# Two mixtures of experts: routing each batch by itself beside the experts of the batch ahead

## The chip, the cores and the metric

The kernel runs on one core of one Trainium2 chip. The metric is the device time of one execution in microseconds (us); three executions of the kernel before took 819.97 us in the median (819.3 to 822.01).

## The reference, cut to what matters

The input is x, four batches of 512 tokens of 128 numbers. Four blocks are added to it in turn, each on a layer norm of x: a test-time-training attention, a mixture of experts, a softmax attention, and the same mixture of experts again. The change is in the two mixtures:

```python
def _L0_ffn_ref(x, We, be, Wg, bg):      # E = 8 experts, K = 2, D = O = 128
    x_flat = x.reshape(-1, d)
    gates = jax.nn.softmax(x_flat @ Wg + bg, axis=-1)
    topk_gates, topk_idx = jax.lax.top_k(gates, K)
    topk_gates = topk_gates / jnp.sum(topk_gates, axis=1, keepdims=True)
    expert_out = jnp.einsum('nd,edo->neo', x_flat, We) + be
    selected = jnp.take_along_axis(expert_out, topk_idx[:, :, None], axis=1)
    out = jnp.sum(selected * topk_gates[:, :, None], axis=1)
...
x = x + _L0_attn_a_ref(_layernorm(x, axis=-1), ...)
x = x + _L0_ffn_ref(_layernorm(x, axis=-1), ...)
x = x + _L0_attn_b_ref(_layernorm(x, axis=-1), ...)
x = x + _L0_ffn_ref(_layernorm(x, axis=-1), ...)
```

## The kernel before, in words

x lies on the chip the whole time, as 16 tiles of 128 tokens (a tile is 128 partitions of 128 numbers), four tiles to a batch. Every product that must be exact in float32 is made of three multiplications (`mm3`, L97 to L102): high part by high part, high by low, low by high. All experts are computed for every token, and each is weighted by a number that is zero for the six that were not chosen.

Each mixture is one call of `moe_phase` (L972 on), a program of its own between two barriers, in which each engine works through a list in the order of the code. It has these stages, each for all 16 tiles before the next begins:

- The norm. VectorE works out mean and inverse root (`ln_vector`, L387) with ScalarE's Sqrt in the middle (`ln_scalar`, L403), 16 tiles at once, then normalizes tile by tile (L1124). TensorE transposes four tiles at a time (L1076), ScalarE takes the high part out of the bank (L1054), VectorE the low part (L1130), and TensorE multiplies by the router's weights into 8 columns a tile (logits, 12 multiplications a batch at L100 to L102).
- The choice. When all logits are there, VectorE adds the bias (L1141), subtracts the largest, ScalarE takes Exp (L1057), and VectorE finds the best and second best by twice four or five operations on all 128 x 128 gates (L1150 to L1163). TensorE computes the experts of tiles 0 and 1 meanwhile.
- The biases. The weights of the experts are transposed (L1099), parted into high and low (L1059, L1165), and multiplied by the experts' biases, a 128 x 2048 matrix that holds them once per tile, into four banks (three multiplications of 512 columns each). VectorE adds each bank to x (L1169).
- The experts. For each tile TensorE does six multiplications of 512 columns into a pair of banks. There are four pairs in the eight banks, and a tile waits until the tile four before has left its pair. VectorE weights and sums experts 0 to 4 from the banks (L1187, five operations a tile, into two sums a and b), ScalarE scales experts 5 to 7 (L1066), GpSimd adds those up (L1043, L1045) and closes the tile with a + b (L1034). In the first mixture VectorE also takes the statistics of each closed tile for the next norm (L385). In the second, SyncE sends each finished batch out.

## Time and profile before

| what | us |
|---|---|
| median of 3 executions (lowest, highest) | 819.97 (819.3, 822.01) |
| the profiled execution's own time | 819.79 |
| its span, from the first to the last instruction | 818.0 |
| first mixture, from its first instruction to the last sum on VectorE | 346.2 to 402.0 |
| second mixture, the same | 760.6 to 814.8 |
| VectorE busy in the whole span | 519.8 |
| TensorE busy in the whole span | 753.3 |

The sum of the prediction is made against the profiled execution. Times within a mixture are told from its first instruction, at 346.2 or 760.6 us of the span. "Busy" of TensorE counts pipelined multiplications and their modelled ends, so it says little of how full the engine is. The granted clock of TensorE is given as a share of 2.4 GHz: 0.50 is the lower of its two levels (1.2 GHz), 1.00 the upper.

### The profile page before, as it was taken

The page shows a single profiled execution, that of the slowest core. Times are in us where ns is not written, and L with a number is a line of the kernel's source. Part 1 is how long each engine was busy: PE and PEld are TensorE (multiplying, and loading weights), DVE is VectorE, ACT ScalarE, POOL GpSimd, SP SyncE. Part 2 cuts the span into 40 slices and gives each one's busy share as a digit, 9 for nine tenths or more (in the row PEclk, how much of TensorE's full clock was granted, in tenths as well). Part 3 has the DMA queues.
Part 4 walks back from the last instruction along what each step waited for, and adds up shares of the span by engine and source line. Part 5 has one row for each costly group of instructions (what it writes and reads, how often), then busy time and mean ns, then how long its engine had stood idle before and what let it go on. Part 6 is the DMA issues. An engine that isn't in the chain of part 4 may idle for free. (4 is left out here: it accounts for less than half of the span.)

```text
span 818.0 us, 15239 instructions
## 1 busy us (share of the span) xinstructions
PE 753.3 (92%) x5432; PEld 601.2 (73%) x5432; DVE 519.8 (64%) x1570; ACT 382.7 (47%) x1080; POOL 266.6 (33%) x465
## 2 busy tenths in 40 slices
PE   5699999979999989888599999999999999999786
PEld 2389999859998878786357667777777777778764
DVE  5755555455555544457877777766766776664477
ACT  4533333543332362213457666655666655663224
POOL 5691000068000011004624444433334333442027
PEclk9799999999999999958889999999999999999679
DMA  8000000000000000000000000000000000000001
GB/s 249 4 0 2 1 1 1 2 0 2 1 1 1 2 1 1 1 1 0 1 1 2 1 2 1 2 2 2 2 2 1 2 1 2 1 2 2 1 0 52
DMA packets 9464, 7.15 MB, mean 9 GB/s; under 512 B 1584, under 2 KB 9008, under 8 KB 9264
## 3 DMA queue, kind: packets, MB, share of 16 engines
q1 hardware_dynamic: 9392, 6.19, 2.5%
q8 instruction: 45, 0.74, 0.4%
q14 instruction: 27, 0.22, 0.1%
HBM read 5.14 MB, written 1.05 MB: 8 GB/s over the span
## 5 line engine op out<-in xcount | busy, mean ns | idle before, releaser
L1324 POOL TENSOR_SCALAR t_p_<-t_p_,t_rinv_ 128x128 f32<-128x128 f32 (+3 forms) x256 | 132.5, 535 | 202.4 <-DVE t_rinv_ L1520 202.4
L1354 ACT ACTIVATE t_p_<-t_p_,t_nmin_ 128x128 f32<-128x128 f32 (+3 forms) x256 | 140.0, 551 | 9.6 <-DVE t_nmin_ L1513 9.6
L1513 DVE CUSTOM_DVE_ANT_0 t_p_<-t_S_,t_mask_ 128x128 f32<-128x128 f32 (+3 forms) x256 | 112.9, 488 | 21.6 <-PE t_S_ L1411 17.3
L1359 ACT ACTIVATE t_pT_<-t_T_ 128x384 f32<-128x384 f32 (+1 forms) x96 | 50.6, 527 | 118.2 <-PE t_T_ L1423 118.2
L1423 PEld LDWEIGHTS t_T_<-ident,t_p_ 128*128 128x128 f32 x640 | 68.2, 141 | 45.0 <-issue 26.1
L1411 PE MATMUL t_S_<-t_k_,t_q_ 64*128 64x256 f32 (+3 forms) x512 | 95.0, 468 | 0.1
L1423 PE MATMUL t_T_<-ident,t_p_ 128*128 128x128 f32 x640 | 90.8, 281 | 0.3 <-ACT t_pT_ L1359 0.3
L1438 PEld LDWEIGHTS t_O_<-t_pT_,t_v_ 128*64 128x64 f32 x1280 | 69.2, 137 | 11.0 <-ACT t_pT_ L1359 10.5
L1438 PE MATMUL t_O_<-t_pT_,t_v_ 128*64 128x128 f32 x1280 | 76.9, 275 | 0.0
L717 POOL TENSOR_TENSOR gvl<-gv,gvh 128x512 fp32r<-128x512 f32 x2 | 2.5, 1274 | 204.3 <-ACT gvh L824 204.3
L1411 PEld LDWEIGHTS t_S_<-t_k_,t_q_ 64*128 64x128 f32 x512 | 41.4, 185 | 26.9 <-DVE t_nmin_ L1513 12.3
L587 DVE SCALAR_TENSOR_TENSOR g_sw<-g_th,g_G 128x512 f32<-128x512 f32 x32 | 22.0, 688 | 59.4 <-ACT g_slope L465 29.9
L1524 DVE COPY t_pT_<-t_T_ 128x384 f32<-128x384 f32 (+1 forms) x96 | 57.3, 597 | 1.4 <-PE t_T_ L1423 1.3
L1529 DVE COPY t_oT_<-t_O_ 128x512 f32<-128x512 f32 x32 | 22.1, 692 | 54.8 <-PE t_O_ L1438 54.8
L1354 ACT ACTIVATION_READ_ACCUMULATOR t_p_<-t_p_,t_nmin_ 128x1 f32 x256 | 48.7, 190 | 0.0
L1066 ACT ACTIVATE m_y_<-m_A_,m_wt_ 128x128 f32<-128x128 f32 x96 | 28.1, 368 | 26.5 <-PE m_A_ L102 26.5
L469 ACT ACTIVATE g_hT<-g_H 128x512 f32<-128x512 f32 x32 | 19.1, 597 | 37.2 <-PE g_H L523 36.4
L610 DVE SCALAR_TENSOR_TENSOR g_du<-g_D,g_sw 128x512 f32<-128x512 f32 x32 | 22.1, 692 | 21.4 <-PE g_D L102 21.4
L530 PEld LDWEIGHTS g_PT<-proj,g_hT 128*128 128x128 f32 x256 | 33.7, 193 | 2.6
L550 PE MATMUL acc<-qkv,g_dg 128*128 128x128 f32 x256 | 34.0, 276 | 1.0 <-DVE g_dg L614 1.0
L530 PE MATMUL g_PT<-proj,g_hT 128*128 128x128 f32 x256 | 34.1, 276 | 0.0
L461 ACT ACTIVATE g_th<-g_G 128x512 f32<-128x512 f32 x32 | 19.1, 598 | 31.4 <-PE g_G L102 31.3
(254 smaller groups left out, 1707.3 us busy)
## 6 DMA issues: line engine op xcount, KB each, us to landing
wqkv<-in_L_attn_b_w_qkv_dram SPq DMA_DIRECT2D x1, 1536.0 KB
x<-in_L_attn_a_x_dram SPq DMA_DIRECT2D x4, 256.0 KB, 3.9
out_dram<-x SPq DMA_DIRECT2D x4, 256.0 KB, 2.3
we<-in_L_ffn_We_dram SPq DMA_DIRECT2D x1, 512.0 KB
wout<-in_L_attn_b_w_out_dram SPq DMA_DIRECT2D x1, 512.0 KB
gv<-n_L_attn_a_ttt_gate_dram SPq DMA_DIRECT2D x1, 256.0 KB, 4.8
gv<-in_L_attn_a_ttt_val_dram SPq DMA_DIRECT2D x1, 256.0 KB, 6.0
proj<-n_L_attn_a_ttt_proj_dram SPq DMA_DIRECT2D x1, 256.0 KB, 4.7
```

The costliest lines, as they stand in the source:

```text
L530: last = pe.matmul(pred, hT[:, t.ring, n * P:n * P + P], self.proj[:, n, :], start=(n == 0), stop=(n == NC - 1))
L550: last = pe.matmul(self.acc[:, n, m, :], src[:, t.ring, m * P:m * P + P], d[:, t.ring, :] if n == 2 else k, start=False, stop=False, skip_ ...
L610: dve.scalar_tensor_tensor(du[:, t.ring, :], psD[:, :], 0.5, sw[:, t.ring, :], ALU.mult, ALU.mult).then_inc(g["du"], 1)
L1066: last = act.activation(y[:, t % 4, tile_of(k)], experts_of(t, e), ACT.Copy, scale=weight(t, e))
L1324: last = pool.tensor_scalar(pr[:, G.par, h, cols], pr[:, G.par, h, cols], rinv[:, G.par, n:n + 1], 1.0, ALU.mult, ALU.mult)
L1354: act.activation(pr[:, G.par, h, cols], pr[:, G.par, h, cols], ACT.Exp, bias=nmin[:, G.par, n:n + 1], scale=-1.0, accum_out=rsum[:, G.par, ...
L1359: act.activation(pT[:, G.par, 0, G.blocks], psT[:, 0, 0:G.width], ACT.Copy).then_inc(t["eA"], 1)
L1411: last = pe.matmul(psS[:, (2 * G.n + h) % 3, at_:at_ + (qt + 1) * P], qp[d, G.par, qt * P:qt * P + P], kp[d, G.par, 0:(qt + 1) * P], start ...
L1423: last = pe.transpose(psT[:, h, k:k + P], pr[:, G.par, h, at_:at_ + P], ident[:, :])
L1438: last = pe.matmul(psO[d, qt * P:qt * P + P], v[:, G.b % 2, n, G.p * P + h * DH:G.p * P + h * DH + DH], pT[:, G.par, h, at_:at_ + P], star ...
L1513: dve.tensor_tensor_reduce(pr[:, G.par, h, cols], psS[:, (2 * G.n + h) % 3, at_:at_ + keys], mask[:, SEQ - keys:SEQ], 1.0, -NEG, ALU.add, ...
L1524: dve.tensor_copy(pT[:, G.par, 1, G.blocks], psT[:, 1, 0:G.width]).then_inc(t["eB"], 1)
```

## The change

`moe_phase` is replaced by `mixture_phase`, which makes a `Router` and an `Experts` object and walks all engines through one table of steps. The router works on one batch at a time: the norm's numbers on GpSimd with the power -0.5 (no Sqrt), the normalization on ScalarE, then transposes, high and low parts, logits, choice, weights and bias product of that batch. The choice goes by rank: all differences between two logits of a token are compared (8 x 8 per token, so 256 numbers a partition for a batch), a sum over them gives each expert's rank, and the shares of ranks 0 and 1 are 0.5 + 0.5 tanh(d/2) and 0.5 - 0.5 tanh(d/2) of the difference d of the two logits. The expert tiles follow FIRST = 7 steps later, one a step, in three pairs of banks; bank 7 is for the router's transposes and logits, bank 6 for weights and bias products. A tile's first half waits now until the tile three before has been summed through expert 3, the second until it has been summed through expert 4 and scaled. The experts' biases are held once per batch (32 x 512).

```diff
+class Router:
+    def norms(self, pool, b, ready):
+        st, w, of = self.k.stats, self.lnw, self.rows(b)
+        pool.wait_ge(*ready)
...
+        c(pool.tensor_tensor(self.rstd[:, of], w[:, 3, of], self.k.mhalf[:, 0:TPB], ALU.pow))
+        pool.tensor_tensor(self.nmr[:, of], w[:, 2, of], self.rstd[:, of], ALU.mult).then_inc(self.s["rstd"], 1)
...
+    def norm(self, act, b):
...
+            last = act.activation(self.xn[:, b % 2, n, :], self.k.x[:, t, :], ACT.Identity, bias=self.nmr[:, t:t + 1],
+                                  scale=self.rstd[:, t:t + 1])
...
+    def choose(self, dve, b):
...
+        c(dve.tensor_tensor(diff, l.unsqueeze(2).broadcast_to([P, TPB, NE, NE]), l.unsqueeze(3).broadcast_to([P, TPB, NE, NE]),
+                            ALU.subtract))
+        c(dve.tensor_tensor(diff, diff, self.k.least[:, :, :].unsqueeze(1).broadcast_to([P, TPB, NE, NE]), ALU.is_ge))
+        c(dve.tensor_reduce(self.rank[:, of, :], diff, AX.X, ALU.add))
+        c(dve.tensor_scalar(self.second[:, of, :], self.rank[:, of, :], 1.0, None, ALU.is_equal))
+        c(dve.scalar_tensor_tensor(self.sign[:, of, :], self.rank[:, of, :], 0.0, self.second[:, of, :], ALU.is_equal, ALU.subtract))
+        c(dve.tensor_tensor(self.second[:, of, :], self.sign[:, of, :], l, ALU.mult))
+        dve.tensor_reduce(self.lead[:, of], self.second[:, of, :], AX.X, ALU.add).then_inc(self.s["lead"], 1)
+        c(dve.tensor_scalar(self.half[:, of, :], self.rank[:, of, :], 2.0, 0.5, ALU.is_lt, ALU.mult))
...
+    def share(self, act, b):
+        act.wait_ge(self.s["lead"], b + 1)
+        act.activation(self.gate[:, self.rows(b)], self.lead[:, self.rows(b)], ACT.Tanh, scale=0.5).then_inc(self.s["gate"], 1)
...
+class Experts:
...
+    def multiply(self, pe, t, before):
+        xh, xl, at = self.r.xh, self.r.xl, slice(t * P, t * P + P)
+        for half in range(2):
+            if before is not None:
+                if half:
+                    pe.wait_ge(self.s["y"], before + 1)
+                pe.wait_ge(self.s["a"], self.sums(before, (3, 4)[half]))
...
-    def moe_phase(self, nth):
+    def mixture_phase(self, nth):
...
+        FIRST = 7
+        STEPS = FIRST + NT + 2
+        STEP = {"norm": (0, 2, 5, 9), "turn": (0, 4, 6, 10), "high": (1, 5, 8, 12), "low": (1, 5, 8, 12), "logits": (1, 5, 8, 12),
+                "choose": (2, 6, 10, 14), "share": (3, 7, 11, 15), "weights": (3, 7, 11, 15), "turn_weights": (3, 7, 11, 15),
+                "weights_high": (3, 9, 13, 17), "weights_low": (4, 9, 13, 17), "biases": (4, 9, 13, 17), "add_biases": (5, 11, 15, 19)}
...
+                for s in range(STEPS):
+                    t = s - FIRST + 2
+                    if 0 <= t < NT:
+                        X.multiply(pe, t, t - 3 if t > 2 else None)
+                    for b in due(s, "turn_weights"):
+                        R.turn_weights(pe, b)
+                    for b in due(s, "biases"):
+                        R.biases(pe, b)
+                    for b in due(s, "logits"):
+                        R.logits(pe, b)
+                    for b in due(s, "turn"):
+                        R.turn(pe, b)
...
+                for s in range(STEPS + 2):
+                    for b in due(s, "add_biases"):
+                        R.add_biases(dve, b)
+                    if 0 <= s - FIRST <= NT:
+                        X.turn(dve, s - FIRST)
+                    for b in due(s, "low"):
+                        R.low(dve, b)
+                    for b in due(s, "choose"):
+                        R.choose(dve, b)
+                    for b in due(s, "weights"):
+                        R.weights(dve, b)
+                    for b in due(s, "weights_low"):
+                        R.weights_low(dve, b)
...
```

At the kernel's start GpSimd clears a quarter of the biases' tile, and fills two small constants (`least`, the smallest positive difference below the diagonal, and `mhalf`, -0.5); SyncE issues 4 loads of the biases in place of 16.

VectorE's list at the choice, first mixture, before (m_A_ are the banks, m_gate_ the Exp of the logits, m_eq_ and m_sel_ the marks of the chosen):

```order
L1141 TENSOR_TENSOR m_logit_<-m_A_,bg 128x128
L1143 TENSOR_REDUCE m_m_<-m_logit_ 128x16
L1144 TENSOR_TENSOR m_logit_<-m_logit_,m_m_ 128x128
L1150 TENSOR_REDUCE m_m_<-m_gate_ 128x16
L1151 TENSOR_TENSOR m_eq_<-m_gate_,m_m_ 128x128
L1152 TENSOR_TENSOR m_eq_<-m_eq_,m_prio_ 128x128
L1153 TENSOR_REDUCE m_pm_<-m_eq_ 128x16
L1154 TENSOR_TENSOR m_sel_<-m_eq_,m_pm_ 128x128
```

and with the change, from the sums of step 10 on (m_diff_ are the differences, m_a_ and m_b_ the two sums of a tile):

```order
L557 SCALAR_TENSOR_TENSOR m_b_<-m_A_,m_wt_,m_b_ 128x128
L423 TENSOR_TENSOR m_logit_<-m_A_,bg 128x32
L426 TENSOR_TENSOR m_diff_<-m_logit_ 128x256
L428 TENSOR_TENSOR m_diff_<-m_diff_,least 128x256
L429 TENSOR_REDUCE m_rank_<-m_diff_ 128x32
L430 TENSOR_SCALAR m_second_<-m_rank_ 128x32
L431 SCALAR_TENSOR_TENSOR m_sign_<-m_rank_,m_second_ 128x32
L432 TENSOR_TENSOR m_second_<-m_sign_,m_logit_ 128x32
L433 TENSOR_REDUCE m_lead_<-m_second_ 128x4
L434 TENSOR_SCALAR m_half_<-m_rank_ 128x32
L475 TENSOR_TENSOR x<-m_A_,x 128x512
L557 SCALAR_TENSOR_TENSOR m_b_<-m_A_,m_wt_,m_z_ 128x128
```

The choice of 19 operations on all tiles, which stood ahead of every sum, is now four choices of 9 operations and 2 for the weights; the first stands ahead of all sums, the second behind none, and the third and fourth between the sums of two tiles.

TensorE's list with the change, from the weights of batch 0 on (ident marks a transpose, beh and bel the biases, weh and wel the experts):

```order
L456 MATMUL m_A_<-ident,m_wt_ 32x128
L100 MATMUL m_A_<-beh,m_wTh_ 128x512
L101 MATMUL m_A_<-bel,m_wTh_ 128x512
L102 MATMUL m_A_<-beh,m_wTl_ 128x512
L398 MATMUL m_A_<-ident,m_xn_ 128x128 x4
L100 MATMUL m_A_<-weh,m_xh_ 128x512
L101 MATMUL m_A_<-wel,m_xh_ 128x512
L102 MATMUL m_A_<-weh,m_xl_ 128x512
```

The transposes of batch 1 stand behind the bias product of batch 0, and the experts of tile 0 between them and the logits of batch 1; before, the transposes of batch 1 followed those of batch 0, and all logits stood ahead of tile 0.

## Rows read from the trace of the kernel before

**Rows 1.** Busy time by stretch: length, PE, PEld, DVE, ACT, POOL, clock, DMA, GB/s.

```profile
346.20:402.90 56.70, 44.47 (x173) 35.60 (x173) 41.15 (x148) 19.71 (x57) 21.85 (x56) 0.74 0.00 1
760.60:815.30 54.70, 44.23 (x173) 35.54 (x173) 39.02 (x132) 19.69 (x57) 21.75 (x56) 0.77 0.05 15
```

**Rows 2.** Timeline, first mixture: start, us, engine, instruction, idle before it.

```profile
349.51 2.14 PE L1076 MATMUL m_A_<-ident,m_xn_ 128*128 128x128 f32 x8 [5.18 <-DVE m_xn_ L1124]
...
352.04 0.38 PE L100 MATMUL m_A_<-wgh,m_xh_ 128*128 128x8 f32 x1 [0.39 <-DVE m_xl_ L1130]
...
363.62 0.35 PE L102 MATMUL m_A_<-wgh,m_xl_ 128*128 128x8 f32 x1
...
363.84 0.77 PE L100 MATMUL m_A_<-weh,m_xh_ 128*128 128x512 f32 x1
...
364.01 0.29 DVE L1141 TENSOR_TENSOR m_logit_<-m_A_,bg 128x128 f32<-128x128 f32 x1 [3.59 <-PE m_A_ L102]
```

**Rows 3.** Timeline, from the choice to the biases, first mixture.

```profile
366.54 0.54 PE L100 MATMUL m_A_<-weh,m_xh_ 128*128 128x512 f32 x1
...
370.11 0.29 DVE L1163 TENSOR_TENSOR m_wt_<-m_sel_,m_rtot_ 128x128 f32<-128x128 f32 x1
370.46 0.48 PE L1099 MATMUL m_A_<-ident,m_wt_ 128*128 128x128 f32 x1 [2.23 <-DVE m_wt_ L1163]
...
371.63 0.80 PE L100 MATMUL m_A_<-beh,m_wTh_ 128*128 128x512 f32 x1 [0.69 <-DVE m_wTl_ L1165]
...
372.65 0.63 PE L102 MATMUL m_A_<-beh,m_wTl_ 128*128 128x512 f32 x1
...
373.07 0.63 PE L100 MATMUL m_A_<-beh,m_wTh_ 128*128 128x512 f32 x1
...
373.31 0.69 DVE L1169 TENSOR_TENSOR x<-m_A_,x 128x512 f32<-128x512 f32 x1 [1.74 <-PE m_A_ L102]
```

**Rows 4.** Timeline in the stage of the experts, first mixture.

```profile
383.06 0.39 PE L101 MATMUL m_A_<-wel,m_xh_ 128*128 128x512 f32 x1
383.28 0.39 PE L102 MATMUL m_A_<-weh,m_xl_ 128*128 128x512 f32 x1
...
387.30 0.28 DVE L385 BATCH_NORM_STATS2 stats<-x 128x6 f32<-128x128 f32 x1
387.50 0.34 DVE L1187 SCALAR_TENSOR_TENSOR m_b_<-m_A_,m_wt_,m_z_ 128x128 f32<-128x128 f32 x1
...
388.79 0.29 DVE L385 BATCH_NORM_STATS2 stats<-x 128x6 f32<-128x128 f32 x1
```

**Rows 5.** Groups with their shapes: busy us, mean ns of one, idle before them.

```profile
L580 DVE TENSOR_TENSOR qkl<-g_PT,qkh 128x256 fp32r<-128x256 f32 x16 | 6.8, 423 | 0.0
...
L1151 DVE TENSOR_TENSOR m_eq_<-m_gate_,m_m_ 128x128 f32<-128x128 f32 x4 | 1.2, 292 | 0.1
...
L836 DVE TENSOR_SCALAR n_aI<-ident 128x128 f32<-128x128 f32 x2 | 0.4, 222 | 0.0
...
L392 DVE TENSOR_TENSOR lnw<-lnw 128x16 f32<-128x16 f32 x4 | 0.7, 176 | 0.1
...
L217 ACT ACTIVATE g_dg<-x,g_nmr,rstd 128x128 f32<-128x128 f32 x16 | 7.7, 488 | 0.8 <-DVE g_nmr L299 0.8
...
L404 ACT ACT_TABLE_LOAD x3 | 3.8, 1283 | 23.2 <-PEq L1243 11.8 <-PEq L877 6.7 <-PEq L1201 4.7
...
L164 POOL TENSOR_TENSOR gvh<-gv,ones 128x1024 fp32r<-128x1024 f32 x1 | 2.4, 2351 | 6.8 <-DMA gv<-in_L_attn_a_ttt_val_dram 6.8
...
L672 POOL TENSOR_TENSOR wgl<-wg,wgh 128x8 fp32r<-128x8 f32 x1 | 0.2, 204 | 0.1
...
L1043 POOL TENSOR_TENSOR m_z_<-m_y_ 128x128 f32<-128x128 f32 x32 | 14.8, 461 | 51.0 <-ACT m_y_ L1066 51.0
```

**Rows 6.** The last sum of each mixture on VectorE, from the timeline.

```profile
401.23 0.74 DVE L1187 SCALAR_TENSOR_TENSOR m_b_<-m_A_,m_wt_,m_b_ 128x128 f32<-128x128 f32 x2
814.02 0.74 DVE L1187 SCALAR_TENSOR_TENSOR m_b_<-m_A_,m_wt_,m_b_ 128x128 f32<-128x128 f32 x2
```

More of the change, by code:

```diff
@@ L1003, in moe_phase @@
-            block_of = lambda g: slice(g * SEQ, g * SEQ + SEQ)
-            tile_of = lambda t: slice(t * P, t * P + P)
-            weight = lambda t, e: wt[:, t, e:e + 1]
-            def experts_of(t, first, count=1):
-                at = (4, 6, 0, 2)[t % 4] + first * P // 512
-                return psAll[:, at, first * P % 512:first * P % 512 + count * P]
-            def sums(t, e):
-                turn = t + LATER[e]
-                here = [k for k in ORDER if 0 <= turn - LATER[k] < NT]
-                return (ON_DVE * turn - 3 if turn else 0) + here.index(e) + 1
+            psAll = c.enter_context(nc.psum_tensor(f"m{nth}_A_", [P, 8, SEQ], F32))
@@ L1086, in experts @@
-                def experts(t):
-                    if t > 3:
-                        pe.wait_ge(s_y, t - 3)
-                        pe.wait_ge(s_a, sums(t - 4, 4))
-                    elif t > 1:
-                        pe.wait_ge(s_xb, BATCH)
-                    for half in range(2):
-                        cols = slice(half * 512, half * 512 + 512)
-                        last = mm3(pe, experts_of(t, 4 * half, 4), xh[:, tile_of(t)], xl[:, tile_of(t)], weh[:, cols], wel[:, cols])
-                    last.then_inc(s_E, 1)
@@ L1097, in biases @@
-                def biases():
-                    pe.wait_ge(s_c, 1)
-                    pe.transpose(psT[:, 0, 0:P], wt[:, :, :].rearrange("p t e -> p (t e)"), ident[:, :]).then_inc(s_wT, 1)
-                    pe.wait_ge(s_wl, 1)
-                    for n, bank in enumerate(banks):
-                        mm3(pe, bank, wTh[:, :], wTl[:, :], beh[:, block_of(n)], bel[:, block_of(n)]).then_inc(s_B, 1)
-                turn(0)
-                for g in range(BATCH):
-                    if g + 1 < BATCH:
-                        turn(g + 1)
-                    logits(g)
@@ L1109, in _ @@
-                experts(0)
-                experts(1)
-                biases()
-                for t in range(2, NT):
-                    experts(t)
+                for s in range(STEPS):
+                    t = s - FIRST + 2
+                    if 0 <= t < NT:
+                        X.multiply(pe, t, t - 3 if t > 2 else None)
[7 more added lines that the diff above has]
+                        R.turn(pe, b)
@@ L1128, in low @@
-                def low(g):
-                    dve.wait_ge(s_xh, g + 1)
-                    dve.tensor_tensor(xl[:, block_of(g)], psT[:, g % 2, :], xh[:, block_of(g)].bitcast(F32),
-                                      ALU.subtract).then_inc(s_xl, 1)
-                norm(0)
-                for g in range(BATCH):
-                    if g + 1 < BATCH:
-                        norm(g + 1)
-                    low(g)
-                wide = lambda ap: ap[:, :].unsqueeze(2).broadcast_to([P, NT, NE])
```

360 lines of the change are left out of this document (211 added, 149 removed).

## The prediction

> **What bounds the kernel now.** I read the busy time by stretch first. The mixtures take 56.7 and 54.7 us, 14% of the span, and in them no engine is full: VectorE is busy 41.2 and 39.0 us of it, TensorE's granted clock is 0.74 and 0.77 in the mean [rows 1]. The timeline shows two parts. In the first 17.8 us of the first mixture (346.2 to 364.0) VectorE waits again and again, at last 3.6 us: norm, transposes and the 48 multiplications for all logits run one behind the other, TensorE at 1.2 GHz, from 352.04 to 363.62, which is about 0.21 us from one small multiplication to the next when the eight transposes in between are taken off [rows 2]. From 364.0 on VectorE sets the pace, in the choice, and then in the sums of the experts, 1.29 us for five operations plus 0.20 for the statistics, that is 0.26 a sum [rows 4]. TensorE needs 6 x 0.23 = 1.4 us a tile there at 2.4 GHz [rows 4]. Between the two lies the stage of the biases, where VectorE waits for TensorE, which the clock has let down to 1.2 GHz: 0.42 us from one 512-column multiplication to the next [rows 3]. The last sums end at 402.0 and 814.8 [rows 6], 55.8 and 54.2 us after the start.
>
> So there are two things to work out: when VectorE now gets work without a gap, and how much work it then has. The time changes by the sum of both, twice.
>
> **The start, batch 0 alone.** Six steps stand one behind the other, in the first mixture as in the second.
>
> - GpSimd's ten operations on 4 numbers a partition. The nearest row is 0.204 us for 8 numbers [rows 5]. Six wait for their forerunner (0.28 with the hop), four don't (0.15): 2.3 us. For the power no row exists: below it costs nothing more than a product, above I allow 1 us, twice a 128-wide operation of GpSimd (0.461) [rows 5], and take 0.2. 2.5 us.
> - ScalarE's four normalizations of 0.488 [rows 5], which overlap a little: 1.7, an estimate under their sum of 1.95. This makes 4.3 with the hop. Before, the transposes began 3.3 after the start [rows 2], so the norm by itself loses 1 us.
> - Transposes to first logit: 2.5, as 349.51 to 352.04 [rows 2]. Twelve small multiplications and the way to VectorE: 11 x 0.21 + 0.39 = 2.7 [rows 2]. 9.5.
> - The choice as far as the difference of logits. The three operations on 256 numbers cost 0.42 by the row at that width, which stands beside 0.292 at 128 [rows 5], plus 0.03 between dependent ones: 1.37. Five around them on 32 numbers lie between 0.176 (16 numbers) and 0.292 (128) [rows 5]; I take 0.19 to 0.2, with the gap 0.22: 1.1. Tanh on ScalarE and back: 0.3. The two for the weights: 0.45. 12.7.
> - Transposed weights, high and low part: 1.2 from the transpose to the first bias multiplication [rows 3]. 14.0. VectorE's addition starts 1.7 later [rows 3] and is done at 16.4.
> - TensorE goes on: two more bias multiplications until 15.4, transposes of batch 1 until 16.5, tile 0 (6 x 0.42 = 2.6 at the low clock, 1.4 at the high), 12 logits (2.6 or 1.3), 0.4 to VectorE. Before, the clock rose 2.7 us after the first of a dense row of 512-column multiplications, 363.84 to 366.54 [rows 2, 3]. The dense row starts here at 14.0, so it should rise within tile 0. I take 2.3 + 1.5. The choice of batch 1 begins on VectorE at 20.6; the bounds are 19.6 and 22.1.
>
> Before, the choice began at 17.8, with all four batches' logits there. **The start costs 2.8 us more**: only a quarter of the logits is on the path now, but behind it stand a choice, a bias product and a second round of transposes, high and low parts, and logits, with TensorE idle in between.
>
> **The work from there.** Per mixture: 3 choices of 2.6 (1.37 + 0.23 + 4 x 0.23, and 0.1 for the one that waits for nothing) = 7.8; 3 pairs for the weights at 0.35 = 1.05; 3 low parts of the weights, 0.2 each = 0.6; 3 bias additions at 0.6 = 1.8; 2 low parts of x at 0.6 = 1.2; 80 sums at 0.258 = 20.6 [rows 4]; 12 statistics before the last sum at 0.20 = 2.4, in the first mixture alone; 0.2 at the end, where two dependent sums stand alone [rows 6]. 35.7 and 33.3 us. Before, 55.8 - 17.8 = 38.0 in the first mixture, waits included: for Exp, for the transposed weights (370.40 to 373.31, 2.9 us with one operation on VectorE in them) and for the bias products [rows 3]. These waits do go. But the choice grows: it took 6.4 us (364.01 to 370.40, with Exp) for 19 operations on all tiles [rows 2, 3], and is 4 x (2.6 + 0.35) = 11.8 now, because 256 numbers are compared for each batch where 128 were for all.
>
> **Waits that are left.** I followed TensorE through the steps. Its ring has three pairs, so tile t starts when the sum of expert 4 of tile t - 3 is done, and from there to the next sum that needs it lie half a tile (0.9 to the last column), ScalarE's three scalings (0.9), and GpSimd's two additions (2 x 0.46 and 0.1 [rows 5]): 2.9 us over two of VectorE's steps. With the statistics two steps are 3.0 and nothing is lost; without them they are 2.6, so in the second mixture each of the last tiles loses up to 0.15. With the bias product of batch 3 this makes 0.5 in the first mixture and 0.8 in the second. TensorE stands idle during the third and fourth choice, by 1.3 and 2.4 us, which costs nothing as long as its clock stays up.
>
> **The sum.** First mixture 20.6 + 35.7 + 0.5 = 56.8, against 55.8: +1.0. Second 20.6 + 33.3 + 0.8 = 54.7, against 54.2: +0.5. What follows a last sum (the closing on GpSimd, the barrier, the output) is unchanged. At the kernel's start GpSimd waits 6.8 us for the weights after its fills [rows 5], which covers the new ones, and the biases are needed late: nothing; without that cover the two new fills and the comparison would cost some 1 us. The Sqrt and Exp loads of ScalarE's tables, 1.283 each [rows 5], lay beside other work: nothing. **+1.5 us**, 821.3 by the profiled execution's 819.79, 0.18 under the median: 821.4.
>
> **The rivals.**
>
> Slower, the ring. For it: before, TensorE fell to 1.2 GHz in the gap of 2.2 us ahead of the transposed weights, with the biases then at 0.42 [rows 3], and my count finds a gap of 2.4 us in each mixture and one of 1.3. Against it: when the clock is down, TensorE has work without a gap, and that raised it before. A fall costs TensorE half the time until the clock is up again, and I allow twice the 2.7 us above, so 2.7, of which its idle time absorbs about 1.5; if each of three gaps a mixture lets it fall, the sums wait about 1 us each: 6 us, 827.4 with the forecast's 1.5. It decides if gaps like those 2.2 us return in the midst of the sums. The Trainium skill ("TensorE: Matmul & The Clock Gate", A second HAM failure mode: psum-queue depth-cycling) says that short idle times between groups, as banks are cycled, let the clock swing and cost throughput; before, with four pairs, the trace disagrees, since the stage of the experts held the high clock.
>
> Slower, the table. If Tanh needs a load after all, 1.283 [rows 5] lies on the path of batch 0, between lead and weights: 822.7 for one mixture, 824.0 for both.
>
> Faster, cheap comparisons. One row, on 128 numbers with both ends in on-chip memory and not in a bank, has 0.222 where 0.292 is the rule [rows 5]. If the 256-wide operations run at half the price, 0.21 instead of 0.42, each choice saves 0.63, four a mixture: -5.0, and 816.4. Against it: the operations of the choice before read no bank either and took 0.292 [rows 5].
>
> **How the numbers follow.** A measurement of this kernel can tell 0.3%, 2.5 us, from no change, so faster is below 817.5 and slower above 822.4. My forecast has 0.5 (0.42 the same, 0.08 slower); the ring 0.2, all slower; the table 0.1, of which 0.07 slower; cheap comparisons or a shorter start 0.2, of which 0.15 faster. That gives 0.15, 0.5 and 0.35. The range goes from 817.0, near the cheap comparisons, to 827.0, near the ring.
>
> **What would show it.** In the profile after: transposes of batch 0 some 4.3 us into each mixture, the second choice at about 20.6, from there no idle time on VectorE beyond 1 us, a 256-wide operation at 0.42, and the last sum at 56.8 and 54.7. A second choice before 18 us or 256-wide operations at 0.3 would make me wrong to the fast side; a granted clock below 0.9 after 22 us, or waits of the sums for GpSimd's or TensorE's results of over 2 us, to the slow side.

## The result, and the profile after

The changed kernel takes 826.6 us in the median (825.5 to 830.0), the kernel before beside it 820.4: a ratio of 1.0086, 95% interval 1.0061 to 1.011 (the two medians alone give 1.0075). It is slower by 0.6 to 1.1%, by 6.2 us in the medians, where +1.5 us was forecast and "no change" was the likeliest case. The profiled execution took 825.81, span 824.1. By stretch (length, busy time of PE, PEld, DVE, ACT, POOL, clock, DMA, GB/s), against [rows 1], and VectorE's last sums, against [rows 6]:

```profile
344.30:404.50 60.20, 42.97 (x176) 31.62 (x176) 41.64 (x149) 23.78 (x76) 32.40 (x87) 0.79 0.00 1
763.00:820.90 57.90, 40.31 (x176) 29.66 (x176) 39.60 (x136) 23.52 (x76) 32.18 (x87) 0.84 0.05 14
```

```profile
403.67 0.81 DVE L557 SCALAR_TENSOR_TENSOR m_b_<-m_A_,m_wt_,m_b_ 128x128 f32<-128x128 f32 x2
```

The first mixture starts at 344.3 and its last sum ends at 404.5, 60.2 us later, where it was 55.8; the second needs 57.8 (763.0 to 820.8) instead of 54.2. That is **8.0 us more in the two mixtures** (8.1 before rounding). The span grew by 6.1 only, since the first mixture starts 2 us earlier. No run shows this to be the change's doing: in the fourteen kernels profiled for this case the last statistics ahead of the first mixture end between 343.3 and 348.5, and with the old code behind them between 344.7 and 347.1. The stretch between the mixtures is 358 to 359 us in every one.

The start chain of the first mixture, from the timeline:

```profile
346.13 1.04 POOL L379 TENSOR_TENSOR m_rstd_<-m_lnw_,mhalf 128x4 f32<-128x4 f32 x1
...
349.18 1.12 PE L398 MATMUL m_A_<-ident,m_xn_ 128*128 128x128 f32 x4 [6.83 <-ACT m_xn_ L389]
351.71 0.38 PE L100 MATMUL m_A_<-wgh,m_xh_ 128*128 128x8 f32 x1 [1.41 <-DVE m_xl_ L407]
...
354.47 0.19 DVE L423 TENSOR_TENSOR m_logit_<-m_A_,bg 128x32 f32<-128x32 f32 x1 [2.81 <-PE m_A_ L102]
...
358.81 0.79 PE L100 MATMUL m_A_<-beh,m_wTh_ 32*128 32x512 f32 x1 [0.67 <-DVE m_wTl_ L466]
...
366.27 0.77 PE L100 MATMUL m_A_<-weh,m_xh_ 128*128 128x512 f32 x1
```

The transposes come 4.9 us after the start (forecast 4.3), the bias product at 14.5 (14.0); the power on four numbers takes 1.04 us, a full microsecond of the chain. Behind the bias product TensorE is never idle, and here is what the forecast had not seen, by window (columns as above):

```profile
344.30:358.80 14.50, 4.24 (x17) 3.45 (x17) 3.70 (x13) 4.25 (x11) 10.79 (x40) 0.53 0.00 1
358.80:369.00 10.20, 10.19 (x32) 8.17 (x33) 3.68 (x11) 3.08 (x9) 0.91 (x2) 0.50 0.00 0
...
777.50:782.00 4.50, 4.44 (x12) 3.30 (x13) 1.39 (x3) 1.71 (x5) 0.00 (x0) 0.50 0.00 0
```

In the first mixture TensorE works for 10.2 us without a gap at the granted clock 0.50 (1.2 GHz) before the clock rises; in the second for 4.5. So tile 0 and the logits of batch 1 all ran at half speed in the first. The second choice begins at 366.45, 22.2 us after the start, and at 20.8 in the second mixture (forecast 20.6). From there VectorE waits little (0.2 us, and 1.4 in the second mixture), yet needs 38.0 and 37.0 us where 36.2 and 34.1 were forecast. The third choice shows a reason, VectorE and GpSimd together:

```profile
374.88 0.43 DVE L426 TENSOR_TENSOR m_diff_<-m_logit_ 128x256 f32<-128x256 f32 x1
374.99 0.63 POOL L516 TENSOR_TENSOR m_z_<-m_z_,m_y_ 128x128 f32<-128x128 f32 x1
375.34 0.56 DVE L428 TENSOR_TENSOR m_diff_<-m_diff_,least 128x256 f32<-128x256 f32 x1
375.59 0.63 POOL L507 TENSOR_TENSOR x<-m_a_,m_b_ 128x128 f32<-128x128 f32 x1
375.94 0.42 DVE L429 TENSOR_REDUCE m_rank_<-m_diff_ 128x32 f32<-128x256 f32 x1
...
376.39 0.41 DVE L430 TENSOR_SCALAR m_second_<-m_rank_ 128x32 f32<-128x32 f32 x1
```

The same operations take 0.43, 0.44, 0.42 and 0.18 us in the first choice, where GpSimd does only four-wide ones. GpSimd's own additions grow too, from 0.46 to 0.63. The choices take 2.6 (first), 2.6, 3.1 and 3.1 us.

### The profile page after: what moved, and what is told of

It is laid out like the page before. It is cut to its first block and busy times, and to the rows that moved or that the text cites. A ratio compares the mean times of both kernels' runs of the same rounds, so it can differ in the third digit from the quotient of the medians.

```text
span 824.1 us, 15420 instructions
## 1 busy us (share of the span) xinstructions
PE 744.0 (90%) x5437; PEld 588.6 (71%) x5438; DVE 521.7 (63%) x1578; ACT 390.7 (47%) x1118; POOL 281.0 (34%) x540
## 5 line engine op out<-in xcount | busy, mean ns | idle before, releaser
L1613 DVE CUSTOM_DVE_ANT_0 t_p_<-t_S_,t_mask_ 128x128 f32<-128x128 f32 (+3 forms) x256 | 112.9, 488 | 21.6 <-PE t_S_ L1511 17.3
L1538 PEld LDWEIGHTS t_O_<-t_pT_,t_v_ 128*64 128x64 f32 x1280 | 69.2, 137 | 11.0 <-ACT t_pT_ L1459 10.5
L1511 PEld LDWEIGHTS t_S_<-t_k_,t_q_ 64*128 64x128 f32 x512 | 41.4, 185 | 26.9 <-DVE t_nmin_ L1613 12.3
L823 DVE SCALAR_TENSOR_TENSOR g_sw<-g_th,g_G 128x512 f32<-128x512 f32 x32 | 22.0, 688 | 58.8 <-ACT g_slope L701 29.9
L1629 DVE COPY t_oT_<-t_O_ 128x512 f32<-128x512 f32 x32 | 22.1, 692 | 54.9 <-PE t_O_ L1538 54.9
L525 ACT ACTIVATE m_y_<-m_A_,m_wt_ 128x128 f32<-128x128 f32 x96 | 28.2, 364 | 26.9 <-PE m_A_ L102 26.8
L100 PE MATMUL m_A_<-weh,m_xh_ 128*128 128x512 f32 x64 | 29.8, 466 | 7.1 <-DVE m_b_ L557 6.9
L846 DVE SCALAR_TENSOR_TENSOR g_du<-g_D,g_sw 128x512 f32<-128x512 f32 x32 | 22.1, 692 | 21.3 <-PE g_D L102 21.3
L697 ACT ACTIVATE g_th<-g_G 128x512 f32<-128x512 f32 x32 | 19.2, 598 | 31.2 <-PE g_G L102 31.1
```

Of the source, the lines that this page charges most:

```text
L100: e.matmul(out, ah, bh, start=start, stop=False)
L525: last = act.activation(self.y[:, t % 4, n * P:n * P + P], self.of(t, e), ACT.Copy, scale=self.weight(t, e))
L1511: last = pe.matmul(psS[:, (2 * G.n + h) % 3, at_:at_ + (qt + 1) * P], qp[d, G.par, qt * P:qt * P + P], kp[d, G.par, 0:(qt + 1) * P], start ...
L1538: last = pe.matmul(psO[d, qt * P:qt * P + P], v[:, G.b % 2, n, G.p * P + h * DH:G.p * P + h * DH + DH], pT[:, G.par, h, at_:at_ + P], star ...
L1613: dve.tensor_tensor_reduce(pr[:, G.par, h, cols], psS[:, (2 * G.n + h) % 3, at_:at_ + keys], mask[:, SEQ - keys:SEQ], 1.0, -NEG, ALU.add, ...
```

## The experiments

Theories for the 8.0 us: (1) the start is a serial chain, and the power and the second round of transposes and logits lengthen it; (2) TensorE's low clock in it is the larger part; (3) VectorE's operations are stretched beside GpSimd; (4) the ring of three pairs makes the sums wait. All times in this table are from each kernel's profiled execution, counted from the end of the last statistics ahead of the mixture (0.3 us before its first instruction).

| kernel | second choice, 1st / 2nd mixture | last sum, 1st / 2nd | both | median, all runs |
|---|---|---|---|---|
| before | one choice | 56.0 / 54.4 | 110.4 | 818.7 |
| changed | 22.5 / 21.1 | 60.5 / 58.1 | 118.6 | 826.6 |
| norm numbers by Sqrt | 19.2 / 20.6 | 58.4 / 58.8 | 117.2 | 827.1 |
| batch 1 earlier | 19.6 / 19.6 | 59.7 / 57.8 | 117.6 | 827.8 |
| one comparison | 22.0 / 20.7 | 60.0 / 56.3 | 116.3 | 825.7 |
| GpSimd busy | 26.9 / 27.7 | 66.1 / 64.6 | 130.7 | 840.5 |
| GpSimd light | 21.9 / 21.6 | 58.2 / 56.6 | 114.8 | 826.7 |
| TensorE filled | 18.6 / 17.6 | 57.0 / 54.8 | 111.7 | 818.6 |
| before, rank on all tiles | one choice | 54.8 / 54.4 | 109.2 | 818.2 |
| before, three pairs | one choice | 56.6 / 55.4 | 112.0 | 822.1 |

(818.7 is the median of the 21 runs of the kernel before that the experiments share; 840.5, 826.7 and 822.1 are single runs, and the stretch ahead of the mixtures differs from run to run by some 5 us, so for them the mixtures' columns are what to read. "Both" is added before rounding; the medians stem from several sittings, in which the kernel before had 818.7 to 820.4.)

**Norm numbers as before.**

```diff
-                    if s < BATCH:
-                        R.norms(pool, s, (self.s_parts, 12))
+                self.ln_scalar(act, R.s["var"], R.s["root"])
+                act.preload_act_table(ACT.Tanh)
...
+                self.ln_vector(dve, R.s["var"], R.s["root"], R.s["ln"])
```

> The changed kernel, but the norm numbers of all batches by VectorE and ScalarE's Sqrt as in the kernel before, the norm of batch 0 by VectorE, and Tanh's table loaded behind the Sqrt; GpSimd has no norm numbers and no power (1.02 to 1.04 us each in the changed kernel). Theory 1 (the start is one serial chain, and all of it lies on the path): the transposes of batch 0 come 3.3 us after the mixture's start instead of 4.9, everything behind them moves up by 1.6, 3.2 us for both mixtures: 823.4 against 826.6. Rival (TensorE's low clock sets the second choice: starting the chain earlier only lengthens the stretch at 1.2 GHz): the transposes move up, the second choice hardly, the time falls by less than 1 us.

The first choice came 1.7 us earlier in the first mixture (8.8 after the statistics, not 10.5) and 1.8 in the second, as theory 1 has it. What became of that differs. TensorE by window (length, busy, clock, DMA, GB/s), from the bias product on:

```profile
360.90:365.00 4.10, 4.10 (x11) 0.50 0.00 0
...
778.10:791.70 13.60, 13.60 (x42) 0.50 0.00 0
791.70:799.00 7.30, 7.30 (x39) 1.00 0.01 3
```

In the first mixture the clock rose after 4.1 us of work without a gap, the second choice came 3.2 us earlier than in the changed kernel and the last sum 2.1; in the second it rose after 13.6, and everything was lost again (0.8 later). The median did not move (827.1; 821.2 to 831.4 over 10 runs). Both mixtures together became 1.4 us shorter, where theory 1 had 3.2. So the time saved at the start, the power's 1 us in it, is real and on the path of the first choice, and smaller than the play of the clock behind it. This run also has the ring rival once, in the midst of the sums of the first mixture:

```profile
386.00:392.70 6.70, 4.64 (x18) 0.98 0.00 1
392.70:395.40 2.70, 2.62 (x8) 0.50 0.00 0
```

The clock fell after TensorE had stood idle for 2.06 us at 389 to 391, and VectorE then waited 1.4 us for a bias product. GpSimd busy (below) has the same once, behind a gap of the same length; the changed kernel itself, batch 1 earlier and the filled kernel have such a gap too, and kept the clock.

**Batch 1 earlier.**

```diff
-        STEP = {"norm": (0, 2, 5, 9), "turn": (0, 4, 6, 10), "high": (1, 5, 8, 12), "low": (1, 5, 8, 12), "logits": (1, 5, 8, 12),
-                "choose": (2, 6, 10, 14), "share": (3, 7, 11, 15), "weights": (3, 7, 11, 15), ...
+        STEP = {"norm": (0, 1, 5, 9), "turn": (0, 2, 6, 10), "high": (1, 2, 8, 12), "low": (1, 3, 8, 12), "logits": (1, 4, 8, 12),
+                "choose": (2, 5, 10, 14), "share": (3, 6, 11, 15), "weights": (3, 6, 11, 15), ...
```

> The changed kernel with the steps of batch 1 earlier: its transposes behind the logits of batch 0, its logits ahead of tile 0, its choice straight behind the first bias addition, its weights in the wait for the first sums. Theory 2 (the second round of transposes, high and low parts and logits on the path is what the start costs): the second choice begins at 18.5 us instead of 22.2 and 20.8, the first sum is then held by TensorE's tile 0 and ScalarE's and GpSimd's part of it, at about 23.2 instead of 24.8 and 23.5; the time falls by 1.6 + 0.6, to 824.4. Rival (VectorE's amount of work alone sets the end): the work behind the first bias addition starts 3.7 and 2.3 us earlier and the end follows: 820.6. Third (the sums wait for TensorE later anyhow): no change, 826.6.

The choice moved up by 2.9 and 1.5 us, the first sum by 2.3 and 1.1 (22.7 after the statistics), the last by 0.8 and 0.3 only, and the median is no better. TensorE worked 9.0 and 7.5 us at 0.50 behind the bias product here, so more of the experts' tiles fell into the low clock. The chain was shortened, and most of it was lost again behind the first sum, where VectorE now waited 1.1 and 1.4 us for GpSimd's sums instead of 0 and 0.6: the third case. That TensorE at half speed is behind these waits is likely, but no run shows it by itself.

**One comparison.** Equal logits are not told apart in this kernel.

```diff
-        c(dve.tensor_tensor(diff, l.unsqueeze(2)..., l.unsqueeze(3)..., ALU.subtract))
-        c(dve.tensor_tensor(diff, diff, self.k.least[:, :, :].unsqueeze(1)..., ALU.is_ge))
+        c(dve.tensor_tensor(diff, l.unsqueeze(2)..., l.unsqueeze(3)..., ALU.is_gt))
```

> The changed kernel with one 256-wide operation less in each choice: the logits are compared directly (greater than), without the difference and the table of least values; equal logits are then not told apart. Theory (VectorE sets the pace in the choices, all four lie on the path): 0.43 us less in the first choice and 0.45 to 0.7 in the others, 2.0 us a mixture, 822.6 against 826.6. Rival (the later choices only fill time in which the sums would wait for the ring): 0.45 + 0.45 a mixture, 824.8.

The second mixture is 1.8 us shorter, near the expected 2.0; the first only 0.5, and there TensorE had its longest stretch at the low clock:

```profile
360.90:374.10 13.20, 13.20 (x41) 0.50 0.00 1
...
779.00:783.80 4.80, 4.80 (x13) 0.50 0.00 0
```

Together that is 2.3 us, nearer to the rival's 1.8 than to the theory's 4.0, and the median fell by 0.9 only. The work saved on VectorE shows in the mixture where the clock rises early, and hardly in the one where it rises late; with two mixtures this is a reading, not a proof.

**GpSimd busy.**

```diff
+                    if s == 1:
+                        pool.wait_ge(R.s["L"], 1)
+                        for n in range(8):
+                            pool.tensor_tensor(fill[:, n, :], self.ident[:, :], self.ones[:, :], ALU.add)
```

> The changed kernel with eight additions of 128 x 128 on GpSimd, to a buffer that nobody reads, beginning when the first logits are there, so that GpSimd works while VectorE makes the first choice. Theory (VectorE and GpSimd are in each other's way where VectorE's operation has both inputs in the on-chip memory): in the first choice the subtraction and the comparison of 256 numbers grow from 0.43 us to 0.55 to 0.75, the sum over 256 numbers (one input) stays at 0.42, GpSimd's additions lie above 0.46 there; each mixture is 0.3 to 1.0 us longer. Rival (the long operations of the later choices come from something else, TensorE's or ScalarE's traffic): the first choice stays at its 2.6 us to the difference of logits, no operation over 0.45.

The first choice beside GpSimd's additions, from the timeline:

```profile
356.66 3.70 POOL L1250 TENSOR_TENSOR m_fill_<-ident,ones 128x128 f32<-128x128 f32 x8 [7.07 <-PE m_A_ L102]
356.84 0.55 DVE L426 TENSOR_TENSOR m_diff_<-m_logit_ 128x256 f32<-128x256 f32 x1
357.43 0.56 DVE L428 TENSOR_TENSOR m_diff_<-m_diff_,least 128x256 f32<-128x256 f32 x1
358.02 0.42 DVE L429 TENSOR_REDUCE m_rank_<-m_diff_ 128x32 f32<-128x256 f32 x1
358.48 0.27 DVE L430 TENSOR_SCALAR m_second_<-m_rank_ 128x32 f32<-128x32 f32 x1
358.78 0.39 DVE L431 SCALAR_TENSOR_TENSOR m_sign_<-m_rank_,m_second_ 128x32 f32<-128x32 f32 x1
```

Theory 3 holds: the two operations with both inputs in the on-chip memory go from 0.43 to 0.55, the small one from 0.19 to 0.39, the sum over one input stays at 0.42. The small comparison with one input (L430) grew too, from 0.18 to 0.27. Not as expected, GpSimd's eight additions keep their 0.46 each. The rule of the Trainium skill ("SBUF — State Buffer", Who interferes with whom) is that a VectorE instruction with two inputs in that memory contends with a GpSimd instruction that reads it, and that a reduction never does: the trace agrees in both halves. How much such an instruction loses the rule does not say; here the two-input operations lost 0.12 to 0.20 us beside additions of 0.46. The mixtures became 5.6 and 6.5 us longer, far more than expected, by an order that I had overlooked in my own edit:

```profile
L445 DVE TENSOR_TENSOR m_sign_<-m_sign_,m_gate_ 128x32 f32<-128x32 f32 x4 | 0.7, 184 | 5.4 <-ACT m_gate_ L439 5.4
```

On ScalarE the normalization of batch 1 stands ahead of the first Tanh and waits for GpSimd's numbers, which now come after the additions.

**GpSimd light.** The output leaves out experts 5 to 7 and the new values, in all but 8 columns.

```diff
-        pool.tensor_tensor(self.k.x[:, t, :], self.a[:, t % 4, :], self.b[:, t % 4, :], ALU.add).then_inc(self.s["x"], 1)
+        pool.tensor_tensor(self.k.x[:, t, 0:8], self.a[:, t % 4, 0:8], self.b[:, t % 4, 0:8], ALU.add).then_inc(self.s["x"], 1)
```

> The changed kernel with GpSimd's additions and closings on 8 columns instead of 128: the output of the mixtures is left without the three last experts and the new values in the other columns, one fill more on GpSimd. Theory (VectorE and GpSimd are in each other's way): in the second, third and fourth choice the operations with two inputs in the on-chip memory are at 0.43 (256 numbers) and 0.19 (32 numbers), a choice takes 2.5 to 2.6 us instead of 3.06, the pair for the weights 0.38 instead of 0.6; the sums (one such input) stay at 0.26; each mixture is 1 to 1.5 us shorter by this, and somewhat more where sums waited for GpSimd. Rival: the long operations stay.

The groups of the three later choices of the first mixture, for the changed kernel and then for this one (mean ns behind the comma):

```profile
L428 DVE TENSOR_TENSOR m_diff_<-m_diff_,least 128x256 f32<-128x256 f32 x3 | 1.4, 470 | 0.1
...
L429 DVE TENSOR_REDUCE m_rank_<-m_diff_ 128x32 f32<-128x256 f32 x3 | 1.3, 420 | 0.1
L446 DVE SCALAR_TENSOR_TENSOR m_wt_<-m_sign_,m_half_ 128x32 f32<-128x32 f32 x3 | 1.1, 370 | 0.1
```

```profile
L428 DVE TENSOR_TENSOR m_diff_<-m_diff_,least 128x256 f32<-128x256 f32 x3 | 1.3, 426 | 0.1
L429 DVE TENSOR_REDUCE m_rank_<-m_diff_ 128x32 f32<-128x256 f32 x3 | 1.3, 420 | 0.1
L446 DVE SCALAR_TENSOR_TENSOR m_wt_<-m_sign_,m_half_ 128x32 f32<-128x32 f32 x3 | 0.6, 194 | 0.1
```

From the second choice to the last sum it takes 36.3 and 34.9 us, 1.7 and 2.1 less than the changed kernel. In the first mixture that is the stretching almost alone, in the second about 0.6 of it are sums that had waited for GpSimd. So theory 3 is worth some 1.5 us a mixture.

**TensorE filled.**

```diff
+                def fill(n):
+                    for _ in range(n):
+                        pe.matmul(psAll[:, 0, :], self.weh[:, 0:P], self.weh[:, 0:512], start=True, stop=True)
...
+                    fill({0: 19, 1: 6, 3: 13, 4: 3}.get(s, 0))
```

> The changed kernel with 41 multiplications of 512 columns, whose result nobody reads, in TensorE's idle time at the start of each mixture (19 ahead of the first transposes, 6 ahead of the logits, 13 ahead of the transposed weights, 3 ahead of the bias product), so that TensorE is never idle there. Theory (TensorE's low clock up to the first sums is what made the start long, and how long it lasts differs from mixture to mixture): the granted clock stays near 1.00 from the mixture's start on, 12 logits take 1.3 us instead of 2.6, the second choice begins at 18.0 to 18.5 us instead of 22.2 and 20.8, the last sum ends 3 to 4 us and 2 to 3 us earlier: 820 to 822 against 826.6. Rival (the work of VectorE and the chain of waits set the start, the clock does not): the fillings keep the clock up, but the time falls by less than 1 us, or rises by what the fillings hold back.

By window, both mixtures, with the second choice at 362.0 and 776.3:

```profile
343.70:348.10 4.40, 4.37 (x12) 3.50 (x13) 0.00 (x0) 1.15 (x3) 3.66 (x16) 0.61 0.00 2
348.10:362.00 13.90, 13.63 (x73) 10.31 (x72) 5.04 (x16) 6.01 (x17) 7.24 (x25) 1.00 0.00 1
...
759.00:776.30 17.30, 16.63 (x84) 12.57 (x85) 5.08 (x16) 7.29 (x19) 10.77 (x40) 1.00 0.00 1
```

No other single edit of the changed kernel is worth as much. Work that nobody needs, on an engine that would wait, brings the clock up within 4.4 us in the first mixture and holds it in the second; the second choice comes 3.9 and 3.5 us earlier, the last sums 3.5 and 3.3, 6.8 us in both mixtures. The median is 818.6, below the 820 to 822 expected and equal to the kernel before (ratio 1.0013, 0.9988 to 1.0038; the changed kernel had 1.0086, so by the ratios it is 6 us). What is left against before is 1.3 us in the mixtures; that this is close to the forecast's +1.5 is chance, since the forecast had counted the low clock of the start in. The low clock was thus worth 6.8 us to the changed kernel. Whether it is why the change lost against before only the same filling of the kernel before can tell, further below.

**Before, with the choice by rank on all tiles.** Exp, 19 operations and their order give way to the rank, the difference and Tanh.

```diff
+                chain(dve.tensor_tensor(diff[:, :, :, :], lj, li, ALU.subtract))
+                chain(dve.tensor_tensor(diff[:, :, :, :], diff[:, :, :, :], least[:, :, :].unsqueeze(1)..., ALU.is_ge))
+                chain(dve.tensor_reduce(gate2[:, :, :], diff[:, :, :, :], AX.X, ALU.add))
...
-                act.preload_act_table(ACT.Exp)
+                act.preload_act_table(ACT.Tanh)
```

> The kernel before with the choice alone of the change: by rank, with Tanh, but on all 16 tiles at once. Three operations on 1024 numbers, by the slope between 128 numbers (0.292 us) and 256 (0.43) 1.2 us each, five on 128 at 0.29, Tanh 0.3, two of 0.3 for the weights: 6.2 us where the old choice took 6.4. Theory (the choice by rank costs only because it is split by batch, four times some 2.9 us): no change, 819.5 within 1 us. Rival (the choice by rank is dear in itself, also on all tiles): over 2 us more a mixture, 824.

```profile
363.11 1.23 DVE L1152 TENSOR_TENSOR m_diff_<-m_logit_ 128x1024 f32<-128x1024 f32 x1
364.37 1.22 DVE L1153 TENSOR_TENSOR m_diff_<-m_diff_,m_least_ 128x1024 f32<-128x1024 f32 x1
```

From the logits to the weights it takes 6.3 us (362.78 to 369.05), as long as the old choice; the ratio to before is 0.9991 (0.9969 to 1.0013). The algorithm costs nothing. Cut into four it takes VectorE 11.4 us in choices alone, and 13.4 with the operations for the weights, which the 6.3 holds too, since an operation on 256 numbers costs 0.43 and not a quarter of the 1.22 for 1024, and the small ones hardly less than before.

**Before, with three pairs of banks.**

```diff
-                at = (4, 6, 0, 2)[t % 4] + first * P // 512
+                at = (4, 6, 2)[t % 3] + first * P // 512
...
-                        pe.wait_ge(s_y, t - 3)
-                        pe.wait_ge(s_a, sums(t - 4, 4))
+                            if half:
+                                pe.wait_ge(s_y, t - 2)
+                            pe.wait_ge(s_a, sums(t - 3, (3, 4)[half]))
```

> The kernel before with the ring of three pairs of banks alone, instead of four. Theory (the ring costs little, since two steps of VectorE cover the way from a freed bank to the next sum but for 0.1 to 0.2 us): the sums of the 16 tiles take 0 to 0.5 us more a mixture, VectorE's waits in them stay under 0.3 us each. Rival (the ring makes the sums wait for TensorE and GpSimd): 1.5 us or more a mixture.

From first to last sum it takes 24.9 and 24.8 us where it took 24.2 and 23.8: 0.7 and 1.0 us for the ring. VectorE's waits in the second mixture (us in total, times, longest):

```profile
DVE m_b_ L1188 <- POOL m_z_ L1045: 1.7, 5, 0.5
```

Five short waits for GpSimd's sum, where before had one of 0.5. That is above the theory's 0 to 0.5 and below its rival's 1.5, and the clock did not fall.

**Which version is fastest.** Four more kernels put the pieces together: the changed kernel with fillings (33), norm numbers by Sqrt and one comparison; that with batch 1 earlier; and the kernel before with fillings, and with the rank choice of one comparison as well.

```diff
+                fill(13)
                 turn(0)
                 for g in range(BATCH):
                     if g + 1 < BATCH:
                         turn(g + 1)
+                    fill((3, 1, 1, 1)[g])
                     logits(g)
                 experts(0)
                 experts(1)
+                fill(16)
```

> The changed kernel with TensorE kept at work at the start of each mixture (33 multiplications that nobody reads), the norm numbers by VectorE and ScalarE's Sqrt, and one comparison in the choice. By the three theories, which would then add up: from the filled kernel alone (the last sums 56.7 and 54.5 us after the mixture's start) 1.7 less for the start and 4 x 0.45 less for the choices, 3.5 us a mixture: last sums at 53.2 and 51.0, the time 811.5. Rival (the earlier start is eaten by TensorE or the ring, as in the runs at the low clock): 815 or more.

> As the one before, and the steps of batch 1 earlier. Theory (with the clock up TensorE's tile 0 no longer holds the first sums back, so the earlier second choice pays now): 1 us a mixture less than without, 809.5. Rival (the weights of batch 0 come 0.5 us later, and nothing is won): the same as without, 811.5 to 812.

> The kernel before with TensorE kept at work in the same way: 13 multiplications ahead of the first transposes, 1 to 3 ahead of each batch's logits, 16 during the choice, 3 ahead of the bias products. Theory (what the change was up against, the start and the biases in series, was itself mostly TensorE's low clock): the choice begins some 13.5 us after the mixture's start instead of 17.8, the bias stage is 1.5 us shorter, 5.5 us a mixture, 808. Rival (the clock falls all the same, or VectorE's norms and low parts bind): under 2 us a mixture, 816 or more.

> The same with the choice by rank on all tiles at once with one comparison (equal logits are not told apart) and Tanh: 1.25 us less for the operation on 1024 numbers that goes, 0.15 less elsewhere: 1.4 us a mixture less than the one before this, 805. It should be the fastest of all: one choice for all batches costs VectorE 4.9 us where four cost 4 x 2.4. Rival: the choice is now shorter than the fillings, which hold the biases back: no gain.

| kernel | last sum, 1st / 2nd | both | median | ratio to before |
|---|---|---|---|---|
| changed, filled, norms, one comparison | 53.6 / 51.0 | 104.5 | 814.2 | 0.9956 (0.9934 to 0.9979) |
| the same, batch 1 earlier | 53.4 / 49.7 | 103.1 | 812.1 | 0.9922 (0.9902 to 0.9942) |
| before, filled | 50.8 / 52.2 | 103.0 | 810.3 | 0.9903 (0.9869 to 0.9937) |
| before, filled, rank and one comparison | 48.1 / 52.7 | 100.7 | 808.6 | 0.9881 (0.9840 to 0.9921) |

With the clock up the pieces add as expected in the mixtures: 3.4 and 3.8 us for norms and comparison, where the same two, one by one, had brought 1.4 and 2.3 us in both together at the low clock. The medians of all four lie 2.3 to 3.6 us above what was expected; of the first, the profiled execution was the fastest of ten, so its mixtures flatter it. Moving batch 1 pays in the second mixture (1.3), hardly in the first (0.2), where the clock was down from 358.4 to 361.8. The kernel before, merely filled, is level with the best of the new design (103.0 and 103.1 us for both mixtures), its choice begins 14.0 and 15.8 us after the last statistics where I had expected some 13.8, and with the shorter choice it has the lowest median: 2.7 us less in its first mixture, 0.4 more in its second. The intervals of the last three overlap, so which of them is fastest is open. VectorE's last sums of the kernel before, filled:

```profile
395.80 0.74 DVE L1196 SCALAR_TENSOR_TENSOR m_b_<-m_A_,m_wt_,m_b_ 128x128 f32<-128x128 f32 x2
805.93 0.74 DVE L1196 SCALAR_TENSOR_TENSOR m_b_<-m_A_,m_wt_,m_b_ 128x128 f32<-128x128 f32 x2
```

This answers theory 2. Filling took 7.4 us from the mixtures of the kernel before (110.4 to 103.0), as much as from those of the changed kernel (6.8). With fillings in both, the change still costs 8.7 us in the mixtures (111.7 against 103.0) and 8.2 in the median. So the low clock is dear to both kernels, but it is not why the changed one is slower. What stays with the fillings is the longer start (its second choice comes 4.5 and 1.8 us later than the one choice of the kernel before) and 1.6 and 0.8 us more from there to the last sum.

The last of the four kernels has a flaw in its second mixture, VectorE's waits, and TensorE by window:

```profile
DVE m_logit_ L1148 <- PE m_A_ L102: 4.4, 1, 4.4
DVE m_wTl_ L1163 <- ACT m_wTh_ L1057: 3.7, 1, 3.7
```

```profile
760.00:761.00 1.00, 1.00 (x9) 0.73 0.00 0
...
773.00:774.00 1.00, 1.00 (x3) 0.50 0.00 0
774.00:775.00 1.00, 1.00 (x5) 0.95 0.00 0
```

The clock was up at the start of that mixture (752.3), fell at 760.5 and was back at 774.1. Tiles 0 and 1 so took 5.3 us on TensorE (767.95 to 773.21) instead of 2.9 in the first mixture; the eleven fillings began only behind them, when the weights were ready, took 3.0 us, and the transposed weights stood behind the fillings: the rival of that run came true in one mixture of two. In the kernel before, filled, the clock was down in the same place, from 763.2 to 773.5. Idle time is not what these falls have in common with those above: TensorE was then busy with the 8-column multiplications of the logits, and had not stood idle for more than 0.4 us since the fillings at the start. A number of fillings that fits both clocks was not tried.

## Why the prediction was wrong

- **What bounds the kernel: right, and more so than I made of it.** I said that the start runs at 1.2 GHz, and costed the change's instructions. Filling shows that the low clock was worth 3.5 and 3.3 us in the two mixtures of the changed kernel, and 5.2 and 2.2 in those of the one before, so next to nothing of the difference between them.
- **The start, batch 0: +0.5 us.** The step "GpSimd's ten operations" took 0.2 for the power. It takes 1.04, the upper bound; the others were a little dear. Transposes to logits (2.5), the 12 logits (2.8) and the first choice (2.6) were right. "The start costs 2.8 us more" is 4.4 and 3.2, from the old choice (17.8 and 17.6 after the start) to the second of the new ones.
- **"The clock should rise within tile 0": a step that failed in the first mixture, by 1.1 us.** It rests on one row pair, 2.7 us from the first of a dense row to the rise [rows 2, 3]; the granted clock itself rose at 366.9, after 3.0. The other mixture of the same trace already had twice that, the kernel before by window, TensorE alone:

```profile
363.80:366.50 2.70, 2.70 (x7) 0.50 0.00 0
778.00:783.30 5.30, 5.30 (x13) 0.50 0.00 0
```

  In the changed kernel it was 10.2 and 4.5, in three of its variants 4.1 and 13.6, 9.0 and 7.5, 13.2 and 4.8. I had bounded the second choice by 19.6 and 22.1; the first mixture came to 22.2, outside: 0.5 from batch 0, 1.1 from the late rise. The second, where the clock rose during tile 0, came to 20.8. Why it rises late in one mixture and early in another stays open. As each late rise leaves TensorE at half speed just where it has work without a gap, this term is not a number but a spread of several us.
- **The work from there, +2.2 us a mixture: the step that failed by most.** "3 choices of 2.6" was measured at 8.7 us for three instead of 7.8, "pairs for the weights at 0.35" at 0.3, 0.6 and 0.6: the prices were those of VectorE alone (the first choice shows them, and the light kernel has them everywhere), and beside GpSimd's additions an operation costs up to 2.4 times as much (0.46 for 0.19). Without those additions the way from the second choice to the last sum was 36.3 and 34.9 us, where I had forecast 36.2 and 34.1. The rest, 0.6 us, are the 512-wide operations that I put at 0.6 where they take 0.69, a number that stood in [rows 3], and the low parts of the weights, 0.27 instead of 0.2. The 80 sums at 0.258 were right; they read one input from a bank.
- **Waits left: 0.5 and 0.8 forecast, 0.2 and 1.4 measured.** The three-pairs run has the ring at 0.7 and 1.0. A small error in the right place.
- **The sum.** Forecast +1.0 and +0.5, measured +4.4 and +3.6. Of the 6.5 us missed, the power and the clock are 1.6 and 0.2 up to the second choice, and 1.8 and 2.9 come after it (stretching about 1.5 each, the underpriced operations 0.6, waits -0.3 and +0.6). So 4.7 of the 6.5 us are work priced too low and its waits, and the clock, which looks like the larger surprise, is the smaller part. The fillings take back more than the late rise alone because they also remove the low clock that I had counted in. The time of 826.6 is inside the range (817 to 827), near its end, but by luck: the case that put the end there, the ring, had another mechanism. (819.97 + 1.5 is 821.5, not 821.4.)
- **The rivals.** The ring: the gaps came (the largest 2.1 us), and in the changed kernel's profile the clock stayed at 1.00 through them, so it is refuted as the cause there. The Trainium skill's rule on cycled banks ("TensorE: Matmul & The Clock Gate", A second HAM failure mode: psum-queue depth-cycling) speaks of frequent short idle times between groups of multiplications. Here it is one gap of 2.06 us in the first mixture of five kernels, and the clock fell 1.4 us after it in two of them, for 3.4 us each (Sqrt and GpSimd busy); VectorE then waited 1.4 and 1.1 us for a bias product. So these traces agree in part. The table: no load stands ahead of Tanh at L439; its four instructions take 0.2 us each, in the first mixture too. Cheap comparisons: the 256-wide ones took 0.42 to 0.44 undisturbed, as forecast.

## What to carry to other kernels

Where a latency-bound chain puts TensorE at its low clock, look at when the clock comes back in every comparable stretch of the trace before building on it, and try the cheap edit first: multiplications that nobody reads, in its idle time, were worth 6.8 us in the mixtures of the changed kernel and 7.4 in those of the kernel before, where the redesign lost 8. And make the cheap edit in both kernels, or it says nothing of why one is slower. Splitting a stage by batch to overlap it multiplies the fixed part of each small operation; the choice with its weights went from 6.4 to 13.4 us a mixture. And work moved beside GpSimd's is not free even on another engine: prices of VectorE's two-input operations must be taken from rows where both are at work.

## What the runs showed of the hardware

- From the first of a dense row of multiplications to the rise of the granted clock from 0.50 to 1.00, 3.0 to 13.6 us passed in the 18 mixtures of the nine kernels without fillings, with much the same instructions ahead of them; 4.1 and 13.6 in one and the same execution.
- The clock also fell without idle time: at 760.5, and at 360.5 and 763.2, in the two filled forms of the kernel before, and at 358.4 in the filled changed one with batch 1 earlier, at or just behind dense 8-column multiplications, with no idle time above 0.4 us in the 6 us before. Behind a gap of 2.06 us it fell in two executions of five.
- GpSimd's power on 4 numbers a partition takes 1.02 to 1.04 us, its other four-wide operations about 0.20.
- VectorE's operations with two inputs in the on-chip memory grow beside a 128-wide GpSimd addition (0.43 to 0.55 to 0.69; 0.19 to 0.39 to 0.46); reductions do not, and sums with one input in a bank do not. A one-input comparison on 32 numbers did too (L430, 0.18 to 0.27 and 0.41).
- VectorE's 256-wide operation costs 0.43 us, the 1024-wide 1.22.
